# Moving two of sixteen shared expert blocks from ahead of the routed blocks to behind them

## What is computed

```python
x = x + attn_a(layernorm(x))
x = x + ffn(layernorm(x))
x = x + attn_b(layernorm(x))      # 16 heads of 8
x = x + ffn(layernorm(x))

def ffn(x):
    probs = softmax(x @ gate_w + gate_b)             # 8 experts
    values, indices = top_k(probs, 2)
    values = values / (sum(values) + 1e-9)
    moe = sum over the two chosen experts of values * mlp_expert(x)
    return x + mlp(x, sh_w1, sh_b1, sh_w2, sh_b2) + moe      # the shared expert
# mlp: gelu(x @ w1 + b1) @ w2 + b2, with 512 inner features
```

## Time and profile before

| | us |
|---|---|
| median of 3 runs | 936.43 |
| lowest, highest | 932.98, 936.88 |
| profiled execution, own time | 932.12 |
| its span, first to last instruction | 930.4 |
| TensorE busy | 698.7 (75%) |
| VectorE busy | 667.8 (72%) |
| ScalarE busy | 521.0 (56%) |
| GpSimd busy | 481.9 (52%) |

### The profile page before, as it was taken

The page is one execution under the profiler, slowest core; times in us unless marked ns, Lnnn a source line. Parts: engine busy times, 40 slices in busy tenths (PEclk is TensorE's granted clock), DMA queues, the critical chain, the costliest instruction groups (busy, mean ns, idle before and its releaser), DMA issues.

```text
span 930.4 us, 24035 instructions
## 1 busy us (share of the span) xinstructions
PE 698.7 (75%) x7840; PEld 553.6 (60%) x7841; DVE 667.8 (72%) x1374; ACT 521.0 (56%) x1212; POOL 481.9 (52%) x463
## 2 busy tenths in 40 slices
PE   1366299799999159999999999994797999995000
PEld 1233299588889135566566566652696888895000
DVE  7888978477775449888888888876785777772222
ACT  3375454466665146877887877774642766662000
POOL 3975446778781777670520300001246788745775
PEclk9998589799999679999999999997698999998555
DMA  6240210233343121010000000000200333341223
GB/s 179 84 75 0 60 33 1 52 86 90 83 87 52 52 62 51 23 49 20 14 14 17 11 17 11 19 7 9 83 1 22 80 84 88 87 69 48 76 75 86
DMA packets 62140, 47.85 MB, mean 51 GB/s; under 512 B 10277, under 2 KB 56265, under 8 KB 62089
## 3 DMA queue, kind: packets, MB, share of 16 engines
q1 hardware_dynamic: 53000, 28.55, 11.1%
q0 software_dynamic: 9088, 18.63, 9.3%
HBM read 26.44 MB, written 16.52 MB: 46 GB/s over the span
## 4 chain that ended last, share of the span: by engine, by line
PE 64%; DVE 14%; POOL 9%; issue 6%; ACT 4%; DMA 2%; SPq 0%; DVEq 0%; ACTq 0%; POOLq 0%
PE ps L680 35%; PE ps L791 11%; POOL gy L629 8%; PE ps L985 7%; DVE xn L1370 5%; PE ps L806 4%; PE ps L998 2%; PE ps L845 2%; DVE hl L1377 1%; PE ps L697 1%; DVE mx L1674 1%; DVE rnorm L1398 1%; ACT scratch L1257 1%; DMA xres<-in_L_attn_a_x 1%; ACT scratch L1127 1%
## 5 line engine op out<-in xcount | busy, mean ns | idle before, releaser
L615 POOL DMA_INDIRECT scratch<-rows,tok_i x156 | 182.9, 1172 | 53.5 <-issue 41.1
L1153 ACT ACTIVATE h<-ps,b1T 128x256 f32<-128x256 f32 x440 | 172.0, 480 | 60.7 <-PE ps L680 60.7
L1674 DVE TENSOR_REDUCE mx<-ps 128x2 f32<-128x512 f32 x256 | 169.6, 685 | 28.9 <-PE ps L680 27.2
L1257 ACT ACTIVATE scratch<-ps 128x512 f32<-128x512 f32 x256 | 148.4, 603 | 46.8 <-PE ps L680 45.5
L629 POOL DMA_INDIRECT gy<-ysorted,slot_i x128 | 121.9, 953 | 75.2 <-DMA ysorted<-yst 37.2
L680 PE MATMUL ps<-xg,w1s 128*128 128x256 f16 x936 | 118.4, 278 | 10.4 <-issue 8.3
L791 PE MATMUL ps<-w2s,hhi 128*128 x1248 | 117.2, 219 | 0.0
L680 PEld LDWEIGHTS ps<-xg,w1s 128*128 x936 | 89.0, 100 | 24.9 <-issue 14.2
L680 PE MATMUL ps<-xn,qst 128*128 128x256 f16 x512 | 97.9, 273 | 6.7 <-DVE mx L1674 5.9
L680 PE MATMUL ps<-hlo,xn 128*128 128x256 f16 x512 | 97.3, 273 | 2.9 <-ACT scratch L1257 2.6
L1523 DVE SCALAR_TENSOR_TENSOR hlo<-h,hhi 128x1024 f16<-128x1024 f32 x78 | 95.6, 1226 | 2.7
(11 more groups left out here) (216 smaller groups left out, 1362.7 us busy)
## 6 DMA issues: line engine op xcount, KB each, us to landing
ysorted<-yst SPq DMA_DIRECT2D x78, 128.0 KB, 1.9
h<-in_L_ffn_ew SPq DMA_DIRECT2D x16, 256.0 KB, 3.2
rows<-hl SPq DMA_DIRECT2D x8, 512.0 KB, 3.5
xn<-kst SPq DMA_DIRECT2D x128, 32.0 KB, 1.8
scratch<-rows,tok_i POOLq DMA_INDIRECT x156, 2.8
xres<-in_L_attn_a_x SPq DMA_DIRECT2D x4, 512.0 KB, 5.9
gy<-ysorted,slot_i POOLq DMA_INDIRECT x128, 2.5
out_x<-xres SPq DMA_DIRECT2D x4, 512.0 KB, 3.3
```

Source lines behind the costliest of these rows:

```text
L615: pool.indirect_dma_start(grow[:, BT * (f % 4) + t, :], None, rows_dram[r], bass.IndirectOffsetOnAxis(ap=tok_i[:, n:n + 1], axis=0))\
L1153: last = act.activation(h32[:, u % 2, f], HB[u % 2][:, f], ACT.Gelu_apprx_tanh, bias=b1T[:, ds(e * CH + c, 1)], scale=1.0 / PS)
L1257: act.activation(prb[:, s % 8, :], ps[:, s % 2, :], ACT.Exp, scale=HD ** -0.5 / (PS * PS))\
L1674: dve.tensor_reduce(mx[:, c, j:j + 5:4], ps[:, 2 + s % 2, :].rearrange("p (n k) -> p n k", n=2), AX_X, ALU.max).then_inc(Att.mx, 1)
```

## The change

Ten shared blocks instead of twelve run ahead of the routed blocks, and six behind. The numbering of group g stands behind `down_shared(g + 2)` instead of `down_shared(g + 4)`, since there are two blocks fewer to stand behind. On VectorE `result_shared(3)` moves from ahead of `onehot(0)` to behind `onehot(1)`; the other results keep their places, and those of blocks 10 and 11 move into the tail with the blocks.

```diff
-    SA = NS - 4
+    SA = NS - 6
...
-                    if 4 <= n < 4 + T // 4:
-                        number(n - 4, n % 2)
+                    if 2 <= n < 2 + T // 4:
+                        number(n - 2, n % 2)
...
-                result_shared(3)
                 for g in range(T // 4):
                     onehot(g, g % 2)
-                    if g >= 2:
+                    if g >= 1:
                         result_shared(2 + g)
```

## The result

| | before | after |
|---|---|---|
| median, us | 934.86 | 944.4 |
| lowest, highest, us | 930.96, 939.57 | 940.47, 947.43 |
| profiled execution, own time, us | 932.12 | 940.47 |
| its span, us | 930.4 | 938.7 |
| TensorE busy, us | 698.7 | 708.3 |

A forecast was written before the change was run, and what follows sets the result against it. TensorE was read as carrying most, with `tok_i` setting when routed blocks start. `tok_i` 4.5 us later in each of two layers plus 0.34 makes 9.3, so 936.43 + 9.3 = 945.7 us; own range 944.1 to 949.0, full range 938.9 to 950.0.

The forecast's parts named there:

- The exchange: Ahead of `number(0)`: two removed blocks become a 6.6 us TensorE wait, gaining 0.34 us per layer, not 6.4.
- TensorE's time truly leaves the path: Rival, at `number(0)`: with routing ready early, each layer gains 3.8 us, giving 929.1 us; chance of faster 0.04.
- The clock: From `number(0)`: after the gap TensorE runs at 1.2 GHz for 3.35 us, losing 1.7 us per layer.
- the clock stays low: Rival, in the numbering steps: short waits keep the clock low, up to 20 us a layer, about 955 us; chance 0.07.
- The loop: `number(1)` to `number(6)`: shared results wait on the block just issued, steps alternate 3.50 and 3.82 us, 0.9 us lost.
- The end: `number(6)` to `tok_i`: `number(7)` and `bexp` to `slot_i` wait behind late shared results, 2.3 us lost per layer.
- The tail: Behind the first layer's routed blocks: `result_shared(15)` before `next_stats` adds 0.34 us; second layer's end unmoved.
- The sum: Whole kernel: 2 x 4.5 us for the layers plus 0.34 for the tail, 9.3 us slower; chance 0.74.

The follow-up runs named there:

- e6: Changed kernel with looped filler matmuls in the gap before `number(0)`, each shared result one `onehot` later, `bexp` to `slot_i` before the last two results; 0.9997 of before.
- e4: Kernel before with ten shared blocks ahead and six behind, but `number(g)` still behind `down_shared(g + 4)`; 0.9955 of before.
- e2: Changed kernel with VectorE reordered: each shared result one `onehot` later, `bexp` to `slot_i` ahead of the last two results; 1.005 of before.
- e9: Changed kernel with each shared result one `onehot` later, `bexp` to `slot_i` still behind the last results; 1.0107 of before, on the slower chip.
- e5: Changed kernel with 56 filler matmuls, as a loop of 14 times four, in TensorE's gap ahead of `number(0)`; 1.0044 of before.
- e12: Repeat of the e10 kernel on another chip, `down_shared(10)` between `number(6)` and `number(7)`; 0.9961 of before.
- e1: Changed kernel with 56 filler matmuls written out in TensorE's gap ahead of `number(0)`; 1.0176 of before.
- e3: Changed kernel with the written-out filler of e1 and the VectorE reordering of e2 together; 1.0102 of before.
- e7: Kernel before, twelve blocks ahead, with `number(6)`, `number(7)` and the end of IDX ahead of `down_shared(10)`, `bexp` to `slot_i` behind the sixth group; 0.9946 of before.
- e11: Kernel of e7 run again beside e12 on one chip; 0.9961 of before.
- e10: Kernel of e7 with `down_shared(10)` put between `number(6)` and `number(7)`, on the slower chip; 0.996 of before.
- e8: Kernel before with fourteen shared blocks ahead and two behind, the end of IDX straight behind `number(7)`; 1.002 of before.

## Why the prediction was right

*The exchange.* Forecast: the wait before `number(0)` is 6.6 us, and the stage gains 0.34 there. Measured 6.63 and 6.64 us, and 0.35. e6 shows that this exchange alone changes nothing in the total that its interval can tell (0.9997 [0.9975, 1.0019]). The rival "TensorE's time truly leaves the path" falls with it, and e4 shows what it would have needed: the numbering must not move.

*The clock.* Forecast: low behind the gap for 3.35 us, a loss of 1.7. Measured 2.6 and 1.5 us; from `number(0)` to the clock's return it is 5.5 and 3.25 us, the first over the upper end (5.1), the second near the mean. With e2 and e9 there are six such steps: low for 3.05 to 5.8 us and 1.4, 1.5, 1.9, 2.2, 2.6 and 2.7 us lost, 2.1 in the mean. So the term was 0.4 too small, and its upper end, 2.55, was passed by two of six. I had taken restarts of routed matmuls, with small turns ahead of them, for one straight out of a gap. That the gap is the cause was argued in the prediction and is shown by e5. The rival "the clock stays low" falls: from `number(1)` on twelve matmuls take 1.47 us. The warning against idle gaps that the prediction took from the Trainium skill ("TensorE: Matmul & The Clock Gate", "Why this matters for your kernels") is borne out here by the 6.63 us gap and the 2.76 us that twelve matmuls took behind it.

*The loop.* Forecast: steps of 3.50 and 3.82 us, 0.9 lost up to `number(6)`. Measured 3.50 and 3.77, 0.8. The term was 0.05 a turn too large: the multiply starts 0.17 and not 0.18 us behind `oneblk`'s end, and the result starts 0.38 behind the bias instead of 0.41. e2 and e9 show the cause by removing it.

*The end.* Forecast 2.3 (2.24 by the prediction's own stepping), measured 1.77. This term was mis-sized too. `number(7)` came 3.50 behind `number(6)`, as forecast, and VectorE had no idle time before `tok_i`. But I took `bexp` at the 1.17 us of the earlier trace rows and kept "0.36 less" only as a bound; it took 0.82. The overlap with a GpSimd multiply decides: here the multiply ran from 164.72 to 166.76, so only 0.47 us of `bexp` lay beside it, and in e9, with none beside it, `bexp` took 0.47 us. I had the shorter overlap in the text and still took the row nearest in place. A further 0.10 is that `tok_i` starts 0.10 ahead of the end of `slot_i` (167.98 against 167.88 + 0.20), where I had added the whole 0.20. With the 0.36 taken off, the step would have been 1.88, close to the 1.77 measured.

*The tail.* Forecast 0.34, measured 0.17: the shared result stands where it was expected, straight ahead of `stats`, but it starts 1.18 us behind the start of `combine(3)`, while `stats` itself in the earlier trace rows starts 1.30 behind it. So 0.21 is added and not 0.33, and `combine(3)` came 0.04 earlier behind the first gather. It waits 3.29 us for its own gather, so the second result ahead of it is covered. The second tail didn't move: from its first gather to the end it takes 86.2 us before and 86.3 after.

*The sum.* 4.84 + 3.77 + 0.17 = 8.8, forecast 9.3; the medians differ by 9.5. That the two agree better than the terms do is partly luck: the clock of layer 0 cost 0.9 more and the end 0.5 less per layer than forecast, and errors of opposite sign cancel in the sum.

*Open.* The attention stage, whose TensorE code is the same in all kernels, took between 344.96 us (before) and 350.27 (e12) on the faster chips, e1 and e3 left aside. The traces place this in its first 42 us: from `stats` to the first matmul at L985 it is 36.7 us before, 36.9 after and 41.6 in e12, and from there to the end of the stage 307.5 to 308.7 in all ten. In e12 the granted clock was low from 35.4 to 42.3 us behind `stats`, and before had no low stretch there after 16.9; but no experiment tests whether that is the cause. `slotb` too, ahead of anything that was changed, comes anywhere from 130.5 to 135.2 us. Such drifts are as large as some of the terms; that is why the terms were read from the stage and not from the totals.

## What to carry to other kernels

Before counting the matmuls that leave a stage, find what the next thing on the engine waits for: here the numberings waited for a routing that was no faster, so 6.4 us of work became 6.6 us of idle time. When an order is written out by hand on several engines, moving one item also changes how far apart the partners of each wait are; a wait on a block two steps back is free, the same wait on the block just issued closes a loop through three engines. A small move did as well as taking blocks out: the last two numberings and the four instructions behind them ahead of the last blocks, with nothing taken out of the front.

## What the runs showed of the hardware

*Instructions written out cost elsewhere.* Fifty-six matmuls in each of two layers, written out, raised the packets of the instruction queue from 31 to 50 and lengthened a looped stage far behind from 345 to 360 us, with issue gaps of up to 3.2 us; the same matmuls as a loop left both as they were. What exactly is loaded again was not settled. A filler in an experiment should be a loop, and the queue's line on the page should be compared before the time is believed.

*A short gap can be followed by a low clock, but not each time.* The prediction weighed gaps of 4.6 us and more. In both layers of e7 and in the second of e11, which is the same kernel, the granted clock fell 1.0 us behind the end of a gap of 1.96 us (16 matmuls in 3.13 us, where high takes 1.95); in the first layer of e11 it stayed high behind the same gap (2.02 us). In e10 and e12, where `down_shared(10)` fills that gap, it stayed high through both blocks in all four layers. In e8 it fell behind gaps of 1.72 and 0.61 us (2.74 us for twelve), though TensorE had been busy with two blocks just before. Behind the 0.57 us ahead of `number(0)` in the earlier trace rows the clock stayed high.

*One chip was slower for all.* On the chip of e9 and e10 the kernel before took 999.46 us instead of some 935, with TensorE waiting for the issue of its own instructions in the routed blocks: 20.6 us in the group of routed matmuls of e9 and 27.9 in that of e10 (the line below), 9.2 in that of after.

```profile
L680 PE MATMUL ps<-xg,w1s 128*128 128x256 f16 x936 | 120.1, 280 | 37.0 <-issue 27.9 <-ACT xg L1183 8.9
```

Apart from the kernel before, one kernel ran both on that chip and on another; it had the same ratio on both (0.996 and 0.9961), though not the same time. Kernels must be compared on one chip.
